# Message passing with counted x rows: the x matmuls of a group in 3 portions instead of 5

## What is computed

```python
h  = x @ node_w.T
rf = edge_attr @ review_w.T
m  = (h[src] + rf) * edge_w                  # one row per edge
agg = segment_sum(m, dst, 12500)
out = layernorm(x + agg, axis=-1)            # eps 1e-5
```

## Time and profile before

| | us |
|---|---|
| median of 2 runs | 2222.93 (2222.28 to 2223.57) |
| profiled execution, its own time | 2227.49 |
| its span, first to last instruction | 2225.4 |
| mean granted TensorE clock | 0.964 |
| busy: DVE | 2025.0 (91%) |
| busy: PE | 1966.0 (88%) |
| busy: ACT | 1576.7 (71%) |
| busy: POOL | 1424.4 (64%) |

### The profile page before, as it was taken

The page is one execution under the profiler, slowest core; times in us unless marked ns, Lnnn a source line. Parts: engine busy times, 40 slices in busy tenths (PEclk is TensorE's granted clock), DMA queues, the critical chain, the costliest instruction groups (busy, mean ns, idle before and its releaser), DMA issues.

```text
span 2225.4 us, 102440 instructions
## 1 busy us (share of the span) xinstructions
PE 1966.0 (88%) x38569; PEld 1731.7 (78%) x38570; DVE 2025.0 (91%) x6186; ACT 1576.7 (71%) x2973; POOL 1424.4 (64%) x1387
## 2 busy tenths in 40 slices
PE   2789989998998999899989998998999899999974
PEld 1578878887887888788878887887888788888864
DVE  4999989998998999899989998998999899999974
ACT  1667767776776777677767776776777677777744
POOL 4776757675767576666757675767576666767300
PEclk7799999999999999999999999999999999999997
DMA  7233333333343333333333333343333334333102
GB/s 144 58 76 86 76 72 76 84 80 77 72 91 66 84 78 82 67 82 85 76 73 76 84 80 78 71 92 71 84 73 82 67 82 85 76 83 74 34 3 59
DMA packets 475430, 169.01 MB, mean 76 GB/s; under 512 B 441312, under 2 KB 453112, under 8 KB 474712
## 3 DMA queue, kind: packets, MB, share of 16 engines
q1 hardware_dynamic: 426794, 111.49, 23.3%
q0 software_dynamic: 44896, 47.21, 10.7%
q10 hardware_dynamic: 3218, 3.20, 0.7%
HBM read 158.58 MB, written 3.20 MB: 73 GB/s over the span
## 4 chain that ended last, share of the span: by engine, by line
PE 53%; DVE 20%; issue 13%; ACT 7%; POOL 3%; DVEq 2%; DMA 1%; ACTq 0%; SPq 0%; POOLq 0%
PE count_ps L1479 23%; PE x_ps L1492 21%; DVE hot_lo L864 11%; PE unit_ps L1404 6%; DVE hot_key L863 6%; ACT counts L1282 3%; POOL rows L540 2%; ACT compared L1257 2%; ACT far_key L1237 1%; DVE sums L778 1%; DVEq L765 1%; PE window_bank L1441 1%; DMA counts<-dst 1%; ACT x_tab L1360 1%; PE window_bank L1433 1%
## 5 line engine op out<-in xcount | busy, mean ns | idle before, releaser
L540 POOL DMA_INDIRECT rows<-x,g_src_cols x1280 | 1326.2, 1036 | 614.1 <-issue 384.5
L1282 ACT ACTIVATE counts<-count_ps 128x588 f32<-128x588 f32 (+1 forms) x1324 | 922.0, 743 | 513.7 <-PE count_ps L1479 509.4
L864 DVE SCALAR_TENSOR_TENSOR hot_lo<-count,cols 128x256 fp32r<-128x256 f16 x2528 | 1168.2, 477 | 1.8
L1479 PE MATMUL count_ps<-hot_key,hot_lo 128*128 128x294 f32 x5056 | 928.9, 320 | 137.8 <-DVE hot_lo L864 54.4
L1479 PEld LDWEIGHTS count_ps<-hot_key,hot_lo 128*128 128x128 f32 x5056 | 724.3, 192 | 238.8 <-ACT counts L1282 75.0
L1492 PE MATMUL x_ps<-counts,x_tab 128*64 128x63 f32 x23716 | 861.8, 225 | 40.9 <-DVE sums L778 39.0
L1492 PEld LDWEIGHTS x_ps<-counts,x_tab 128*64 128x64 f32 x23716 | 779.9, 138 | 110.0 <-DVE sums L778 53.0
L863 DVE TENSOR_SCALAR hot_key<-count,cols 128x294 fp32r<-128x294 f16 x1926 | 737.8, 383 | 63.5 <-PE count_ps L1479 49.8
L1239 ACT ACTIVATE hot_key<-far_key,all_ones 128x294 fp32r<-128x294 f16 x602 | 326.1, 542 | 19.6
L1237 ACT ACTIVATE far_key<-count,neg_key 128x294 f16<-128x294 f16 x602 | 316.3, 525 | 0.1
L1404 PE MATMUL unit_ps<-rows,g_hot 128*32 128x64 f32 x5120 | 95.2, 230 | 0.0
(11 more groups left out here) (199 smaller groups left out, 782.3 us busy)
## 6 DMA issues: line engine op xcount, KB each, us to landing
rows<-edge_attr SPq DMA_DIRECT2D x196, 512.0 KB
rows<-x,g_src_cols POOLq DMA_INDIRECT x1280
out<-x_tab SPq DMA_DIRECT2D x12, 256.0 KB
counts<-dst SPq DMA_DIRECT2D x1, 928.0 KB
a_stage<-dst SPq DMA_DIRECT2D x19, 48.0 KB
a_stage_w<-edge_weight SPq DMA_DIRECT2D x19, 48.0 KB
g_stage<-src SPq DMA_DIRECT2D x20, 32.0 KB
g_stage<-dst SPq DMA_DIRECT2D x20, 32.0 KB
```

Of the source, the lines that this page charges most:

```text
L540: pool.indirect_dma_start(out=g_x[:, i, t, :], out_offset=None, in_=x, in_offset=bass.IndirectOffsetOnAxis(ap=g_src_cols[at.p][:, k:k + 1] ...
L864: dve.scalar_tensor_tensor(hot_lo[h][:, :, :], count16[:, 0:P].unsqueeze(1).to_broadcast([P, 2, P]), cols_[:, LO, j:j + 1], cols_[:, W_LOW ...
L1282: act.activation(to, count_ps[(g + e) % 2][:, 0:n, 0:KEYS].rearrange("p a (h d) -> p a h d", d=D), ACT.Copy).then_inc(counts_read, 1)
L1479: done = pe.matmul(count_ps[(g + e) % 2][:, k % 2, 0:KEYS], hot_lo[h][:, i, :], hot_key[h][:, :], start=(i == 0), stop=(i == 1))
```

## The change

The constants that place the x portions, the units' sums and products on PE change, and with them the places of add_g and make_a_hot on DVE. PORTIONS_AT has 3 entries, so sum_x gets 32, 33 and 33 values of hi instead of 19 or 20. SUM_G goes from 4 to 5, MULTIPLY_G from 8 to 12, SUM_A stays at 12, MULTIPLY_A goes from 16 to 19, TURN stays at 8, where no portion stands any more.

```diff
-PORTIONS_AT = (4, 8, 12, 16, 20)
-SUM_G, MULTIPLY_G, SUM_A, MULTIPLY_A, TURN = 4, 8, 12, 16, 8
+PORTIONS_AT = (5, 12, 19)
+SUM_G, MULTIPLY_G, SUM_A, MULTIPLY_A, TURN = 5, 12, 12, 19, 8
...
-                        if k == 15 and has_g:
+                        if k == 18 and has_g:
                             add_g(at, g)
                             if later_g:
                                 make_g_slot_hot(*next_unit(at, g, GATHERED))
-                        if k == 18 and later_a:
+                        if k == 19 and later_a:
                             make_a_hot(*next_unit(at, g, SUMMED))
```

## The result

The changed kernel takes 2373.49 us (median of 2 runs, 2372.63 to 2374.36) against 2222.93: ratio 1.067, 95% interval 1.064 to 1.070. That is 150 us slower, where I had forecast 38.

The account below looks back on a forecast made before the run. DVE was taken to set the time, with PE close behind. Waits for compare (25.6 us), take_src (11) and the other edits (2) sum to 38.6 us on 2222.93, giving 2261 us; own range 2245 to 2276, overall range 2229 to 2291.

Parts of the forecast that it names:

- step 0, ordinary: DVE's `less` in find_rows waits longer for ACT's compare, behind the moved block: 1.6 us in each of 11 rounds.
- step 0 after a restart: Same compare chain after a loop restart, partly at PE's lower clock: 1.0 us (0.7 to 1.5) in 8 rounds.
- step 1: take_src before window 14 waits for turn_g and read_g: 0.6 us in each of 19 rounds, 11 us.
- steps 2 to 5: No term of their own beyond 2 us for the other edits; steps 4 and 5 keep 17.5 and 15.7 us.
- a longer wait for compare: Step 0: `less` waits about 2 us in ordinary rounds and 2.4 after restarts.
- the new wait of take_src: Step 1, before window 14: a new g_src_cols entry of some 0.6 us a round.
- The other edits, at nothing: Fewer switches, moved add_g, a_hot and products, DVE's windows 11 and 18: covered, 2 us in all.
- These two are thin: DVE's window 18 needs window 12 counted, cover 0.4 us; window 11 needs 5, cover 0.1 to 0.3: 2 us together.
- rival A: PE with ACT bounds every step with sum_g, chain 16.95 us; 26 us more, 2288 us; chance 0.16.
- B: Rival: PE is the bound after all, fewer blocks save 48 us by fewer switches, 2175 us; chance 0.06.
- C: Rival: compare moves but DVE catches up as its later waits shrink, 2223 to 2232 us; chance 0.12.
- D: Rival: longer unbroken matmuls after a restart bring the higher clock back sooner, 10 us off, 2251 us; chance 0.04.

Follow-up runs that it names:

- e3: Kernel before with three portions, before windows 4, 12 and 20, units at their old places: 2267.3 us, ratio 1.020.
- e15: Changed kernel with portions before 4, 12, 20, sum_g before 4, multiply_a before 20, DVE's order as changed: 2307.2 us, 1.037 against the kernel before.
- e1: Kernel before with five portions kept, only the units' sums and products and add_g, a_hot at their new places: 2318.3 us, ratio 1.043.
- e2: Kernel before with three portions, before windows 5, 12 and 19, units at their old places: 2287.7 us, ratio 1.029.
- e13: Kernel before with make_a_hot before window 19 instead of 18, nothing else: 2246.9 us, ratio 1.010.
- e14: Kernel before with add_g and g_slot_hot before window 18 instead of 15: 2239.3 us, ratio 1.006.
- e9: Changed kernel with ACT reading only the lower half of the hi values of each pair of windows: 2286.5 us, 1.027 against the kernel before.
- e16: Changed kernel with 20 values of hi in each portion instead of 32 or 33, all places as changed: 2242.9 us, 1.009 against the kernel before.
- e4: Changed kernel with seven hot buffers instead of six: 2361.2 us, 1.062 against the kernel before.
- e7: Changed kernel with find_rows before window 20 instead of 12: 2376.9 us, 1.069 against the kernel before.
- e12: Kernel before with find_rows before window 20 and four rounds in a pass of the hardware loop instead of two: 2178.1 us, ratio 0.978.

## Why the prediction was wrong

**The sum of the places.** From the kernel before to e3 (three longer portions alone) it is 44 us, from e3 to e15 (DVE's order and the units beside the portions) 40, from e15 to the changed kernel (the places 5 and 19 in place of 4 and 20, the units with them) 66. These make up the 150 along one way through the runs; e1 shows that the same part can cost something else in other company.

**The sum by steps.** Forecast against what rounds 1 to 18 show (the table of means above):

| term | forecast, us | measured, us |
|---|---|---|
| step 0, ordinary | 11 x 1.6 = 17.6 | 32 in 10 rounds |
| step 0 after a restart | 8 x 1.0 = 8 | 26 in 8 |
| step 1 | 11 | 30 |
| steps 2 to 5 | within the 2 for all other places | 49 |
| sum | 38.6 | 137 |

The other 13 us lie outside these rounds.

**What held.** The bound before (DVE), a longer wait for compare, and the new wait of take_src. `less` waits 1.83 us, as I had "about 2 us in ordinary rounds"; after restarts too, where I had 2.4 (and my own times there, 308.5 against 307.64, give +0.9 and not +1.0). I had sum_g of step 1 about 1 us after add_x; it is 1.3 (1111.40 against 1110.06), and take_src waits 0.76 us in each round where I had taken 0.6. The run nearest to my terms is e2, which has the portions at 5, 12 and 19 and nothing else: there step 0 grows by 1.9 us, after a restart by 2.6, and step 1 by 0.65, where I had 1.6, 1.0 and 0.6. Still e2 loses 64 us and not 38.

**The step that failed** is "The other edits, at nothing": first, "These two are thin, and for both I add 2 us over all rounds (0 to 25)", DVE's windows 11 and 18, for which I had written down a cover of 0.1 to 0.4 us. They are the waits of 0.75 and 0.78 us above in step 3 of every round, and the like of them stand in steps 0, 1 and 5: together 87 us of waiting, where the kernel before has no wait before either window. They also belong to step 0, whose chain I had followed only to `less`: behind it DVE waits again before 18, 0.4 us at a granted clock of 1.00 and 1.9 us in the rounds in which the clock fell, a fall that no term of mine had. The sign that I had set for rival A, a step 3 above 16.5 us, came (17.7), and steps 4 and 5 did not keep 17.5 and 15.7 (18.2 and 15.9). I had priced rival A's chain at 16.95 us a step and then set it aside, because "the steps with preparations on DVE (1, 2, 4) and those without sum_g give the lead back". It measures 17.71 in step 3 (1147.40 to 1165.11), by my pieces:

| piece | reckoned | measured |
|---|---|---|
| first block (sum_g, 64 records) | 3.3 | 3.05 |
| windows 5 to 11 | 2.4 | 2.71 |
| second block | 3.0 | 3.02 |
| windows 12 to 18 | 2.4 | 2.78 |
| third block | 2.35 | 2.34 |
| windows 19 to 4 | 3.5 | 3.81 |

The first block was 0.25 us shorter than reckoned, the other two right, and each run of windows was 0.3 to 0.4 us short. I had taken 0.64 us for a reading of a pair, the distance of two that follow one another; a reading on which PE waits costs its whole 0.78 us and the handing over (ACT begins one at 1161.88, PE goes on at 1162.69, 0.81 us later). My sum stood 0.8 us above DVE's own 16.15, and the measured one stands 1.56 above it, about double. The preparations do give the lead back in steps 2 and 4, where hot_key has no wait worth a line, but steps 0, 1, 3 and 5 lose it anew: a lead is at most six windows, and what DVE has once waited is not made up.

Second, the a_hot and add_g moves were looked at only for their semaphores. They cost about 19 us without any (the estimate above; 21 and 13 us each alone): before every third window DVE pauses for its own last result, and what stood there as a filler was moved away.

**The rivals.** A was the right mechanism with a price too low (2288) and too small a chance (0.16); my range ended at 2291 because of that price. B and C are out: no step got shorter. D is out: the stretch at 0.50 after a restart is as long as before (6.8 us in six rounds and 10.2 in two, in either kernel), a second one came behind compare, and the mean granted clock fell from 0.964 to 0.957. The Trainium skill (Perfetto Trace Analysis, Matmul Optimizations) wants matmuls in back-to-back batches. Here the batches became longer, and PE waited more between them, 187.5 us for ACT's readings instead of 26.5, since what fed it was bounded by two pairs of banks.

**Open:** how the 66 us of the places divide between the split pair at 5 and ACT's tail behind 19, since no run moved one of the two places alone; what e13 and e14 cost together, for which there is only an estimate; and in which rounds the clock falls behind compare.

## What to carry to other kernels

When two engines run within a few per cent of the third, reckon the whole ring through buffers and banks, with the full latency of each handing over, and not only the busy engine's own waits: a cover of 0.1 to 0.4 us is no cover. Cut filler work at the buffers' own grain (here pairs of windows, and every third window on DVE), and before moving an instruction on the busy engine look at what pause it fills now. If easing either of two resources gives most of a loss back (e9, e16), and the wait comes up again elsewhere when one edge is opened (e4, e7), that speaks for a ring. Two fillers that go to the same pause, or that swap pauses, don't cost the sum of what each costs alone. And where two runs of one step differ by a fixed amount, look at the granted clock of each.

## What I had not expected of the hardware

An engine's wait for its own previous instruction doesn't show in the list of waits, but costs 0.12 us each time (0.91 against 0.79 us from the start of a pair of hot_lo), and the hot_key behind it at times runs for 0.52 us instead of 0.37 (in the kernel before, for window 0 in 44 of 103 cases). In the changed kernel the granted clock fell to 0.50 for 3.4 us behind a wait of PE of 1.6 us, in 13 of the 19 rounds with a compare, and in the other six it did not. A restart of the hardware loop costs about 8 us of step 0 (24.9 against 16.8); twice as long a body cost no more (24.0 against 16.2 in e12): with 3 instead of 8 restarts e12 saved 48 us, of which about 4 are find_rows.
